# The value products of a slot issued behind the expert products instead of ahead of them, in a two-layer transformer kernel on one core

## What is computed

```python
x = x + L0_attn(ln(x)) + L0_ffn(ln(x))
# L0_attn: softmax(mask(q k^T / sqrt(8))) v, 16 heads, causal
# L0_ffn:  sum over the two chosen experts e of gate_e * (relu(x W1[e] + b1[e]) W2[e] + b2[e])
x = x + L1_attn(ln(x)) + L1_ffn(ln(x))
# L1_attn: ctx = .7 * mha4(x) + .3 * mha16(x); ctx = .85 * ctx + .15 * mha4(ctx); ctx Wo + bo
# L1_ffn:  h = silu(x w1) * (x w2); gelu(gelu(h h1) h2) w3
```

## Time and profile before

| | us |
|---|---|
| median of 3 runs | 1724.08 |
| lowest and highest run | 1718.03, 1724.44 |
| profiled execution, whole | 1719.99 |
| its span, first to last instruction | 1717.8 |
| TensorE busy | 1517.5 (88%) |
| VectorE busy | 1183.1 (69%) |
| ScalarE busy | 1050.0 (61%) |
| GpSimd busy | 784.2 (46%) |

### The profile page before, as it was taken

How to read it: one execution, slowest core, us unless ns; L and a number is a source line. 1 busy time by engine, 2 the same in 40 slices (tenths; PEclk the granted TensorE clock), 3 DMA queues, 4 the chain that set the end, 5 groups by cost and what they waited for, 6 DMA issues and landing times.

```text
span 1717.8 us, 33661 instructions
## 1 busy us (share of the span) xinstructions
PE 1517.5 (88%) x11497; PEld 652.7 (38%) x11497; DVE 1183.1 (69%) x3135; ACT 1050.0 (61%) x2322; POOL 784.2 (46%) x725
## 2 busy tenths in 40 slices
PE   4696788989899999999899999999899999889878
PEld 1352442345333543345333543345333533232232
DVE  6644588567876789667886788567975677477522
ACT  2461665667667766677567765677566765726542
POOL 5245445534645455355654565354654461511120
PEclk9997799999999999999999999999999999979977
DMA  7633740236212631145213621245213720201010
GB/s 279 205 99 106 219 120 27 64 108 171 64 41 81 177 87 52 61 119 160 64 41 93 178 80 48 71 141 125 67 37 93 191 77 10 62 13 38 1 37 7
DMA packets 138873, 159.32 MB, mean 93 GB/s; under 512 B 15745, under 2 KB 100305, under 8 KB 137809
## 3 DMA queue, kind: packets, MB, share of 16 engines
q1 hardware_dynamic: 134608, 148.79, 29.9%
q0 software_dynamic: 4096, 8.40, 1.7%
HBM read 115.96 MB, written 40.85 MB: 91 GB/s over the span
## 4 chain that ended last, share of the span: by engine, by line
PE 62%; DVE 14%; ACT 9%; issue 6%; DMA 4%; SPq 3%; POOL 2%; ACTq 0%; DVEq 0%; POOLq 0%
PE banks L467 59%; DVE negmax L892 7%; ACT probs L1236 3%; ACT hm L1305 3%; DMA qkc<-relm 2%; DVE h L1117 1%; PE banks L744 1%; ACT L1236 1%; SPq L1593 1%; DMA relq<-halves 1%; PE banks L697 1%; DVE h L1112 1%; DVE r_b L1142 1%; ACT h L1354 1%; PE banks L592 0%
## 5 line engine op out<-in xcount | busy, mean ns | idle before, releaser
L1236 ACT ACTIVATE probs<-banks 128x512 f32<-128x512 f32 (+3 forms) x1216 | 581.4, 536 | 377.4 <-PE banks L467 373.1
L892 DVE TENSOR_REDUCE negmax<-banks 128x1 f16<-128x512 f32 x768 | 492.5, 685 | 140.3 <-PE banks L467 137.5
L888 DVE CUSTOM_DVE_ANT_0 scr<-banks,mask_row 128x384 bf16<-128x384 f32 (+3 forms) x512 | 230.2, 487 | 147.6 <-PE banks L467 145.6
L467 PE MATMUL banks<-kp,qs 32*128 32x512 f16 (+3 forms) x1024 | 242.4, 358 | 51.5 <-DVE negmax L892 23.9
L467 PE MATMUL banks<-probs,vp 128*32 128x512 f32 (+3 forms) x2048 | 238.4, 539 | 0.5 <-POOL probs L1409 0.5
L467 PE MATMUL banks<-qs,kp 32*128 32x512 f16 (+3 forms) x1024 | 209.9, 350 | 17.0 <-ACT probs L1236 12.7
L1497 POOL TENSOR_TENSOR h_lo<-h,h_hi 128x512 f16<-128x512 f32 x96 | 112.8, 1190 | 222.2 <-ACT h_hi L1348 136.5
L1437 POOL TENSOR_TENSOR hl<-hm,hh 128x512 f16<-128x512 f32 x120 | 139.7, 1166 | 157.0 <-DVE hh L1059 157.0
L1305 ACT ACTIVATE hm<-banks,wt 128x128 f32<-128x128 f32 x480 | 137.3, 373 | 73.0 <-PE banks L467 72.5
L467 PE MATMUL banks<-qkc 97*128 97x512 f16 (+1 forms) x512 | 167.5, 399 | 10.5 <-DVE negmax L892 3.8
L467 PEld LDWEIGHTS banks<-kp,qs 32*128 32x128 f16 x1024 | 65.3, 92 | 257.3 <-DVE negmax L892 101.1
(11 more groups left out here) (217 smaller groups left out, 2434.9 us busy)
## 6 DMA issues: line engine op xcount, KB each, us to landing
wt<-wexp SPq DMA_DIRECT2D x120, 258.0 KB, 3.1
wt<-wexp SPq DMA_DIRECT2D x120, 256.0 KB, 3.4
qkc<-relm SPq DMA_DIRECT2D x96, 128.0 KB, 3.3
qs<-relq SPq DMA_DIRECT2D x64, 128.0 KB, 2.3
kp<-relk SPq DMA_DIRECT2D x64, 128.0 KB, 2.7
relm<-halves SPq DMA_DIRECT2D x32, 256.0 KB, 2.2
xg<-xslots SPq DMA_DIRECT2D x24, 256.0 KB, 3.0
yslots<-yv SPq DMA_DIRECT2D x24, 256.0 KB, 3.6
```

Source lines behind the costliest of these rows:

```text
L467: return nc.tensor.matmul(psum[rows_, bank, cols_], lhsT, rhs, start=start, stop=stop)
L888: v.tensor_tensor_reduce(scr[:, s, 0:kw], psum[:, SCO + s, 0:kw], mask_row[:, T - kw:T], -1.0, 3e38, ALU.add, ALU.min, negmax[:, g.n % 2, ...
L892: v.tensor_reduce(negmax[:, g.n % 2, NC * h + c:NC * h + c + 1], psum[:, SCO + s, 0:kw], AX.X, ALU.max, negate=True).then_inc(sem("max"), 1)
L1236: a.activation(keys(g, c)[:, 2 * pair + s, q0:T], psum[:, TRA + s, q0:T], ACT.Exp, scale=SCALE[main(g)]).then_inc(sem("exp"), 1)
```

## The change

In TensorE's body of a slot the call of `value` is moved behind `few_cols` and `experts`. No instruction is added or taken away, and the order of the other engines and of SyncE's DMAs is the same.

```diff
                     few_rows(G)
+                    few_cols(G)
+                    experts(G)
                     if G in VALUE_AT:
                         value(*VALUE_AT[G])
-                    few_cols(G)
-                    experts(G)
                     ffn(G, 0)
```

## The result

The changed kernel takes 1737.36 us (median of 4 runs, 1736.39 to 1745.77), against 1723.98 us for the kernel before (4 runs, 1718.03 to 1724.44). The ratio is 1.0114, with a 95% interval of 1.0083 to 1.0146: slower. The medians themselves are 13.4 us apart, a factor of 1.0078. The profiled execution took 1736.39 us with a span of 1734.2, which is 16.4 us more than before. The forecast was 1742 us, in a range of 1726 to 1758.

What follows compares the result with a forecast made beforehand. TensorE was taken as the bound, with the value step as filler before late products. Hidden stalls 20.0 plus form changes 7.5 less gains 6.4 gave +21.1 us, from 1721.2 to 1742 us, range 1726 to 1758.

Steps and rivals of the forecast that it cites:

- The bound and the direction: TensorE bounds the kernel; the value step is filler before late products, so moving it costs time, +21.1 us in all.
- slot 24's stall: Slot 24: `up` waits for ScalarE's copy `xt`, 0.34 us stalled in seven batches, 2.4 us.
- Part 1: Stalls the value step hid in slots 16, 18, 34, 50, 58: 20.0 us; slot 58 costs 0.89 us, seven times.
- nothing there makes that up: Slot 58: VectorE's next awaited product, the gate product, comes 0.89 us later, and none of that is recovered.
- Slot 50: Slot 50: `positions` can't move forward; VectorE's backlog covers some, 0.67 of 0.99 us reach the path, six batches, 4.0 us.
- Slots 16, 18 and 34: New stalls for `xt`, `hl` and bank M: 0.60 us five times, 0.66 and 0.31 us seven times each.
- Part 2: TensorE's whole stream: array form changes rise from 1,613 to 1,688, 75 at 0.10 us, 7.5 us.
- Part 3: Even slots, as slot 22: earlier `up` and `hm` save 0.55 us at 16 L697 waits, 8.8 us; net 6.4 us.
- Part 4: Engines waiting for the value step: no cost summed; GpSimd's late key sums, slots 50 to 56, leave 1.8 us open.
- (a): New stalls vanish in TensorE's waits for VectorE's row maxima: 1722 us, up to 1732; chance 0.17.
- (b): The experts' chain is the hidden bound, so earlier `up` makes the kernel faster: 1712.6 us; chance 0.06.
- (c): Slot 50's late value step breaks GpSimd's chain, slot 56 stalls: +6 to 9 us, 1750; chance 0.15.

Runs made afterwards that it cites:

- forms: Kernel before with the value step put last in slots 12, 20, 38 and 42 alone; one run, 1718.2 us.
- late2230: Kernel before with the value step put last in slots 22 and 30 alone; 1713.48 us, ratio 0.996.
- after_same: The changed kernel, unchanged, run again in another group beside the kernel before; 1736.85 us, ratio 1.0106.
- five_first_again: Changed kernel with the value step put back first in slots 16, 18, 34, 50 and 58, second timing; 1709.46 us, ratio 0.9952 to the kernel before.
- five_late_again: Kernel before with the value step put last in slots 16, 18, 34, 50 and 58 alone, second timing; 1746.12 us, ratio 1.017.
- before_same: The kernel before, unchanged, run and traced again in another group; 1719.98 us.

## Why the prediction was right, step by step

**The bound and the direction.** Filler in front of late operands was taken away, and the late operands did not come sooner. TensorE's waits went up at the five places where that was forecast; elsewhere small ones did (0.27 and 0.21 us for the maxima ahead of slot 53's scores, 0.19 in slot 41, and in slot 32 0.74 instead of 0.44 for a DMA, a wait that also differs between two traces of the same kernel: 2.9 and 1.5 us in all). Predicted for the whole was +21.1 us; the traces say +17.5 for the five steady periods and +16.4 over the span in the first pair, 14.0 and 11.2 in the second, the medians +13.4 and +17.6, and the ratios +18 to +20. The mechanism was right, and the sum lies a little above all of these. That it came so near is in part luck: slots 52 and 53 were not in it and the terms of slots 16, 18 and 34 were too small, while the cost of slot 24's stall did not come and the gain ahead of slot 80 had not been counted.

**Part 1, slot 58** (forecast 0.89 a time): 0.97 less 0.17. The step "nothing there makes that up" failed by a fifth: the gate product of slot 59 had a wait for `h` of its own, of which 0.17 could go. Over seven batches 5.6 us instead of 6.2.

**Slot 50** (forecast 0.99 less VectorE's backlog of 0.32, that is 0.67): 1.00 less 0.29 in the slots 50 and 51, that is 0.71. The cover was the one named. But the place costs 0.49 more in the slots 52 and 53, through GpSimd and VectorE's `gates`, so that it is 1.19 a period and 7.1 us over six batches instead of 4.0. Part 4 had followed GpSimd's late start to the product that needs its sums, and not to what runs beside it.

**Slots 16, 18 and 34** (forecast 0.60, 0.66 and 0.31, with 0.10 each for a change of form counted in part 2, so 0.70, 0.76 and 0.41): 0.82, 0.82 and 0.64. Two things were too small. TensorE starts 0.14 us after ScalarE's `xt` ends (959.46 + 1.03 = 960.49, start 960.63), and 0.15 after VectorE's `vc` (997.92, 998.07); I had allowed 0.06 and 0.02. The right figure could have been read in the earlier trace rows: `xs` ends at 858.49, the product starts at 858.63. After GpSimd's `hl` it is 0.05 (966.28, 966.33). After VectorE's `h` in slot 59 it is 0.06 too (867.84, 867.90), so the short figure exists as well; which one holds has to be read at the place. And a change of form costs rather 0.15 than 0.10. Slot 18 paid in full five times, not seven, and 0.54 us once. Together 13.2 us (4.1, 4.6 and 4.5) instead of 11.7.

**Part 2, changes of form** (0.10 each): 0.11 to 0.19 in the four places of `forms`. The Trainium skill ("TensorEngine Tiling (Array Packing)", Key Properties) says that a change of mode drains the engine. The trace agrees in so far as each change costs time, with these numbers; that it is a drain, no run here shows. Of their sum, 0.22 in slot 40 was not paid, which was not foreseen.

**Part 3, gains** (0.55 a time, 8.8 us at L697): slot 23 -0.57; the waits fell by 8.6 us in the whole change and 7.3 in `late2230`. The stall of slot 24 came as forecast, 0.34 us, but its cost of 2.4 us did not: slot 25 got 0.35 back. The reason is a chain that I had not followed one step further. `up` of slot 25 waited 0.17 us for the `hm` of slot 24's `up`, before:

```profile
971.45 0.83 PE L467 MATMUL banks<-xt,wt 128*128 128x128 f16 x12 [0.17 <-ACT hm L1305]
```

From one `up` to the next it was 2.17 us before (969.28, 971.45) and 2.15 after (977.74, 979.89). The value step of slot 24 now stands between them, in a place where TensorE would have waited; the stall in front of the first `up` was paid with it.

**Part 4** (0 in the sum, 1.8 us left open): no product starts later for the keys' sums, and the slack of 0.99 shrank by the 0.67 us that were worked out, to 0.32, of which the weight load needs nearly all. Putting it at 0 was wrong all the same: GpSimd's lateness cost the 0.49 us a period of the slots 52 and 53, 2.9 us.

**What was not in the sum.** The first slots, up to slot 80, are 3.6 us shorter (5.5 in `after_same`, 4.5 in `five_first_again`, 2.0 in `five_late_again`, 0.4 in `before_same`). Of that 1.1 us stand ahead of slot 19, where the first value step comes and where the kernels are the same, so they are no effect of the change. From slot 19 to slot 80 it is 77.8 us before, 77.9 in `before_same`, 77.8 in `five_late_again`, but 75.3 and 74.7 in the two traces of the changed kernel and 74.1 in `five_first_again`. So a gain of 2.5 to 3.7 us goes with the places outside the five; I did not follow it to an instruction, and its cause stays open. And the granted clock: TensorE had it at 0.5, its lower level of 1.2 GHz, for 138 us in all before and 145 after. Two stretches of the changed kernel show how much that disturbs a single slot (columns: stretch, length, busy us of each engine, granted clock, DMA share, GB/s):

```profile
842.00:850.00 8.00, 7.06 (x42) 2.35 (x35) 7.03 (x17) 5.89 (x15) 7.10 (x5) 1.00 0.22 75
1035.30:1043.30 8.00, 8.00 (x33) 1.90 (x26) 5.36 (x12) 4.51 (x13) 7.07 (x5) 0.57 0.22 75
```

Both begin 0.8 us behind the start of `positions` in slot 50 of their period, with the same wait of 1.35 us for `r_b` just before. In 8 us the first gets 42 of TensorE's products and 17 of VectorE's instructions done, the second 33 and 12. In the second the clock fell behind that wait for 6.8 us; in three of the five steady periods of this trace it did so, in `after_same` in two. Slots 52, 58, 59 and 60 differ by up to 1.9 us from one period to the next with that, and the mean over periods would put 0.8 us of give-back into slots 59 and 60, most of which was low clock in the trace of before.

**The rivals.** (a) The waits for `negmax` fell by 3.3 us, not by the 20 of part 1: false. (b) The gain at L697 was there, but the five places cost more; `late2230` shows that it can be had alone. (c) did not happen: the product of slot 56 is not delayed. But GpSimd's lateness, from which (c) starts, did cost TensorE time, in the slots 52 and 53.

## What to carry to other kernels

Work whose operands are ready long before is worth most directly in front of work whose operands are late; ask of each such step not whether it could stand later, but what the instruction behind it is waiting for at that moment. One rule for all slots is wrong twice here: the value step belongs first in five slots of eighty and last in at least two, and a kernel that keeps the five is 0.3 to 0.5% faster than before where the uniform change is 1.1% slower. When a new stall is costed, follow the next wait of the same chain too: in slot 24 the stall was paid back one slot later, in slot 58 a fifth of it. And when a change delays an engine off the chain, ask what will run beside its work now: here that cost 0.49 us a period where no one waits for the delayed result.

## What the runs showed of the hardware

TensorE's product starts either 0.05 to 0.06 or 0.14 to 0.15 us after the end of the instruction it waits for, and which of the two goes with the place and not with the engine alone: in the traces of both kernels it is 0.14 to 0.15 after ScalarE's `xt` and `hm` and VectorE's `xs`, `vc` and `r_b`, and 0.05 to 0.06 after VectorE's `h` and GpSimd's `hl`, and mostly so after VectorE's `negmax` and ScalarE's `probs`. A value step placed so that a slot has a change more between 32-row, 32-column and full form costs 0.11 to 0.19 us of TensorE's stream.

VectorE's `gates` (L1004, two operands, 32 columns) takes 0.21 us beside GpSimd's one-operand cast `halves`, and 0.75 to 0.78 us when GpSimd's addition or product of two operands (`w<-r_a,r_b`, 1.27 us) has begun 0.56 us earlier; it then ends 0.05 us behind it. It is so in slot 52 of six periods in every kernel with a late value step in slot 50, and in none of these six in `forms`, `five_first_again` and the two traces of the kernel before. The first sequence, ahead of slot 1, has the same pair in every kernel, and there `gates` takes 0.82 to 0.83 us. What the two engines share, no run here shows.

In two of the four groups of runs VectorE took TensorE's scores in slot 50 1.6 to 1.7 us after the scores' start instead of 0.43 (1034.45 to 1036.06, and 1029.06 to 1030.73), ScalarE its own 1.4 us after theirs (1029.38 to 1030.80), while standing idle, in every kernel of the group and in most periods; slot 67 was 0.8 to 1.2 us longer as well. The kernel before took 1741 to 1742 us in these groups and 1719 in the others. The instructions are the same, so it is a property of the chip or the session; each group ran on another chip and at another time, so no run says of which. It makes single runs from different groups useless for a comparison, while the ratios within a group held: 1.0036 for slot 50's term with it, 0.9968 and 0.9952 for the same kernel with and without it.
